# The front of layer 1's attention: waits, loads and order in one engine's list

## What is computed

```python
x = x + _L0_ffn_ref(...)                       # each token: one expert's output, times its weight
y = _L1_cond_ref(x, f, f, w, u, cond)          # sigmoid(x) * (num / den) * (0.8 + 0.2 * tf)
qkv = y @ w_attn + b_attn                      # 16 heads of 32, causal softmax
x = x + (att @ v) @ w_proj + b_proj
```

## Time and profile before

| | us |
|---|---|
| median of 3 runs (2532.3 to 2535.91) | 2533.44 |
| the profiled execution | 2525.72 |
| its span, from first to last instruction | 2524.0 |
| mean granted TensorE clock in it | 0.922 |

### The profile page before, as it was taken

The page is one execution under the profiler, slowest core; times in us unless marked ns, Lnnn a source line. Parts: engine busy times, 40 slices in busy tenths (PEclk is TensorE's granted clock), DMA queues, the critical chain, the costliest instruction groups (busy, mean ns, idle before and its releaser), DMA issues. The chain is left out here.

```text
span 2524.0 us, 43575 instructions
## 1 busy us (share of the span) xinstructions
PE 2093.1 (83%) x14585; PEld 1307.1 (52%) x14585; DVE 1767.6 (70%) x3446; ACT 1355.4 (54%) x3223; POOL 1101.9 (44%) x759
## 2 busy tenths in 40 slices
PE   0678888999999999999995669956789898966999
PEld 0355555565565565566663635533456666643444
DVE  7788877888888878887663449844567767754770
ACT  4566655555555555655553524315476767646442
POOL 5566646555565555554442046633232223210440
PEclk9989988999999999999998579987689899988999
DMA  4233223222122212221122864445333333337110
GB/s 164 80 99 94 80 81 110 76 74 77 60 83 89 70 59 72 78 93 59 56 64 85 334 248 144 144 170 159 102 126 114 102 120 102 118 112 257 34 46 21
DMA packets 112540, 268.53 MB, mean 106 GB/s; under 512 B 10752, under 2 KB 40832, under 8 KB 109824
## 3 DMA queue, kind: packets, MB, share of 16 engines
q1 hardware_dynamic: 93264, 217.50, 25.5%
q10 hardware_dynamic: 16560, 40.64, 4.9%
q0 software_dynamic: 2560, 8.39, 0.9%
HBM read 182.60 MB, written 76.55 MB: 103 GB/s over the span
## 5 line engine op out<-in xcount | busy, mean ns | idle before, releaser
L830 PE MATMUL ps_q<-a_y,a_w 128*128 128x512 f16 x1536 | 356.8, 382 | 0.0
L616 POOL TENSOR_TENSOR a_rb<-a_rb,a_rot 128x512 f32<-128x512 f32 x129 | 187.5, 1454 | 309.0 <-ACT a_rb L729 309.0
L830 PEld LDWEIGHTS ps_q<-a_y,a_w 128*128 128x128 f16 x1536 | 149.8, 102 | 163.8 <-issue 6.1
L620 POOL TENSOR_TENSOR a_qk<-a_ra,a_rb 128x512 f32<-128x512 f32 x129 | 204.6, 1586 | 18.9 <-POOL a_rb L616 0.5
L257 DVE TENSOR_TENSOR_SCAN wkv_bwd<-wk_decay,wkv_tail,wkv_fwd 128x512 f32<-128x512 f32 x114 | 198.5, 1763 | 0.1
L880 PE MATMUL ps_g<-a_o,a_wo 128*128 (+1 forms) x768 | 177.8, 381 | 13.3 <-POOL a_o L607 10.7
L847 PE MATMUL ps_s<-a_qk 128*128 128x512 f32 (+3 forms) x512 | 173.2, 460 | 15.3 <-POOL a_qk L620 15.3
L839 PEld LDWEIGHTS ps_v<-a_w,a_y 128*128 128x128 f16 x3072 | 176.9, 98 | 15.1
L869 PE MATMUL ps_o<-a_tt_,a_v 128*128 128x512 f32 (+3 forms) x512 | 174.6, 488 | 11.1 <-ACT a_tt_ L747 9.5
L839 PE MATMUL ps_v<-a_w,a_y 128*128 128x128 f16 x3072 | 182.0, 219 | 0.0
L968 DVE TENSOR_REDUCE a_nmax<-ps_s 128x1 f32<-128x512 f32 (+3 forms) x256 | 124.7, 487 | 72.1 <-PE ps_s L849 65.4
(11 more groups left out here) (271 smaller groups left out, 4938.6 us busy)
## 6 DMA issues: line engine op xcount, KB each, us to landing
a_w<-wqkv_split SPq DMA_DIRECT2D x48, 768.0 KB, 4.7
scratch_numlog<-wkv_nl ACTq DMA_DIRECT2D x40, 512.0 KB, 2.9
wkv_kt<-in_fT ACTq DMA_DIRECT2D x59, 256.0 KB, 2.7
a_wraw<-in_wqkv SPq DMA_DIRECT2D x18, 768.0 KB, 5.4
wqkv_split<-a_w SPq DMA_DIRECT2D x17, 768.0 KB, 6.8
a_stacks<-qk_parts SPq DMA_DIRECT2D x102, 128.0 KB
gate_up<-in_gate_up SPq DMA_DIRECT2D x8, 1408.0 KB, 14.2
a_nlc<-scratch_numlog SPq DMA_DIRECT2D x18, 512.0 KB, 4.5
```

The costliest lines, as they stand in the source:

```text
L616: pool.tensor_tensor(rb[:, n, :], rb[:, n, :], rot[:, 2 * n + 1, :], ALU.mult).then_inc(s["roped"], 1)
L620: pool.tensor_tensor(qk[:, n, :], ra[:, n, :], rb[:, n, :], ALU.add).then_inc(s["q_sb"], 1)
L830: mm = pe.matmul(psq[n][:], w16[:, i % 2, wp, n, c, :], y16[:, yp, c, :], start=c + m == 0, stop=c == CC - 1 and m == 2)
```

## The change

Four edits, all in `layer1_attn`. The wait for `fixed` and `bq` move from the top of DVE's list to behind the four chunks. `nl0` is loaded in four DMAs, one for each chunk, each with its semaphore, and `xm` is issued behind the first of them. The four first y go to four places (in `ef`), so that `condition` of chunks 1 to 4 no longer waits for `ylo`. In the heads, `weigh` goes ahead of the maxima, and `add_moved` of the tile goes into the next head, behind its maxima.

```diff
+        first_nl = [k.sem(f"a1_first_nl{c}") for c in range(CC)]
...
+        def yf_of(n):
+            return ef[:, 1 - n // 3, n % 3] if isinstance(n, int) and n < CC else yf[:]
...
                 sp.dma_start(x3[:], d["x1"][0].rearrange("c p n -> p c n")).then_inc(s["x1_first"], 16)
-                take_x1(1)
-                sp.dma_start(nl0[:], d["numlog"][2, 0].rearrange("c p m n -> p c m n")).then_inc(s["first_nl"], 16)
+                for c in range(CC):
+                    sp.dma_start(nl0[:, c], d["numlog"][2, 0, c]).then_inc(first_nl[c], 16)
+                    if c == 0:
+                        take_x1(1)
                 sp.dma_start(bqk[:], d["bqkv1"]).then_inc(s["fixed"], 16)
...
-                    pool.tensor_tensor(y[:, 1, c, :], yf[:], y[:, 0, c, :], ALU.subtract).then_inc(s["ylo"], 1)
+                    pool.tensor_tensor(y[:, 1, c, :], yf_of(n), y[:, 0, c, :], ALU.subtract).then_inc(s["ylo"], 1)
...
-                    act.activation(y_of(n)[:, 0, c, :], yf[:], ACT.Copy).then_inc(s["yhi"], 1)
+                    act.activation(y_of(n)[:, 0, c, :], yf_of(n), ACT.Copy).then_inc(s["yhi"], 1)
...
                     if isinstance(n, int) and n < CC:
-                        dve.wait_ge(s["first_nl"], 16)
+                        dve.wait_ge(first_nl[n], 16)
...
                     dve.wait_ge(s["inv"], n + 1)
-                    if not (isinstance(n, int) and n == 0):
+                    if not isinstance(n, int) or n > CC:
                         dve.wait_ge(s["ylo"], n)
-                    conditioned(dve, yf[:], numlog(n)[:, 0, :], wkv_at(b, c), sg[:, side, :]).then_inc(s["yf"], 1)
+                    conditioned(dve, yf_of(n), numlog(n)[:, 0, :], wkv_at(b, c), sg[:, side, :]).then_inc(s["yf"], 1)
...
-                dve.wait_ge(s["fixed"], 48)
-                dve.tensor_scalar(bq[:], bqk[:, 0, :], SCALE, None, ALU.mult).then_inc(s["bq"], 1)
                 weigh(0)
                 for i in range(TT):
                     weigh(i + 1)
...
                     condition(n, n % 2, 0, n)
+                dve.wait_ge(s["fixed"], 48)
+                dve.tensor_scalar(bq[:], bqk[:, 0, :], SCALE, None, ALU.mult).then_inc(s["bq"], 1)
                 take_v(0, 0)
...
+                            if first and h < 2 * TT:
+                                weigh(2 * TT + h)
                             maxima(h + 1, i + 1)
+                            if first and 0 < h <= 2 * TT:
+                                add_moved(2 * TT + h - 1)
...
-                            if first and h < 2 * TT:
-                                weigh(2 * TT + h)
-                                add_moved(2 * TT + h)
```

More of the change, by code:

```diff
@@ L1607, in layer1_attn @@
             "x1_first", "x1_here", "weighted", "moved", "x2", "x2_stored", "wp_raw", "wp64", "wp_hi", "wp_lo",
-            "fixed", "biased", "first_nl", "x_loaded", "sig_step", "sig", "lsum", "inv", "yf", "yhi", "ylo", "y_here",
+            "fixed", "biased", "x_loaded", "sig_step", "sig", "lsum", "inv", "yf", "yhi", "ylo", "y_here",
             "bq", "qproj", "q", "q_hi", "kproj", "k", "k_hi", "qk_low", "parts_out", "stacked", "vproj", "vf", "vhi", "vlo", "scores", "nmax", "expd",
```

## The result

| us | before | after |
|---|---|---|
| median, 4 runs each (2532.3 to 2535.91; 2495.51 to 2509.32) | 2533.38 | 2505.53 |
| the profiled execution | 2525.72 | 2509.32 |
| its span | 2524.0 | 2507.6 |
| mean granted clock | 0.922 | 0.921 |

The ratio is 0.9903 (95% interval 0.9882 to 0.9923, given in brackets from here on): 27.9 us faster by the medians. The two profiled executions differ by 16.4 us only, so the time is followed in them first; what lies between the two numbers comes at the end of the experiments.

The account below looks back on a forecast made before the run. The last stage, from about 1676 us, was taken as the bound: DVE's early waits and PE's waits before moves in the heads. 2525.72 − 8.4 − 0 − 11.2 = 2506.1, plus 7.7 to the median: 2514 us, range 2505 to 2524.

Parts of the forecast that it names:

- The front: Last stage's beginning: weighting starts at 1687.3 in place of 1696.53, so ACT starts the first y 8.4 us earlier.
- `bq` behind the chunks: DVE's wait for the small loads, moved behind the fourth `condition`, near 1710.4: loads landed 14 us before, cost 0.
- Four loads: Division terms in four DMAs: avoids a 0.5 us wait of their first reader, costs nothing; bounds 0 to 3 us lost.
- Four places: Four places for y remove `condition`'s wait for POOL, at most 1.37 us once; taken as 0, bounds 0 to 1.4 gained.
- Head 1's stall: PE's 5.88 us stall ending at 1758.32, covered also by the weight piece and POOL's half: gain 0.
- The other heads: Six other PE waits before moves, 18.1 us at most: gain 11.2 us, middle of 6.4 and 15.9, range 3 to 18.
- Weighting beside POOL's work: Moved weightings in the heads may meet POOL more or less often: 4.1 us later to 2.5 earlier; mean of 795 ns kept.
- Heads gain nothing: Rival: in the heads `values` waits for the addition as long as moves waited for weighting; 2525 us, chance 0.10.
- The clock rises: Rival: PE's clock rises over heads 1 to 8, 10 us more gained; 2504 us, chance 0.06.
- Slower: Rival: waits for the addition keep PE at 1.2 GHz through the eight heads; 2543 us, chance 0.03.
- front fails: Rival: split loads delay gathers or terms by some 8 us at the stage's beginning; 2522 us, chance 0.03.
- The sum: Whole kernel: profiled execution 2525.72 falls to 2506.1; 7.7 us added for the runs' median gives 2514 us.

Follow-up runs that it names:

- the second: The changed kernel run again with nothing edited: median 2504.75 us over 6 runs, ratio 0.9899 against the kernel before.
- the front alone: Changed kernel with weighting and addition back at the end of the head; `bq` late, four loads and four places kept: median 2520.93 us, ratio 0.9958.
- the two profiles above: Two profiles of the changed kernel with the addition at the end of the head: head 3 took 11.21 us at clock 0.54, 9.09 at 0.81.
- the fillers: 24 unread PE multiplications per head in heads 1 to 7, added to the kernel with late `bq`, four loads, four places and old head order: 2524.69 us.
- The two kernels with another place for the addition: Changed kernel with the addition at the end of the head (2500.04 us), or ahead of weighting and maxima in the next head (2497.52 us).

## Why the prediction came out

The forecast was 2514 us, range 2505 to 2524, faster with 0.94. Measured were 2505.5 and 2504.8: faster, by 0.5 us inside the range and by 0.2 outside it. The direction and the mechanisms were right, and two terms were sized too small; that the first median still lies in the range is luck: the range allowed 1 to 2 us for the runs' scatter, and the six runs of the second alone spread over 15.

- **The front, 8.4 us.** ACT came to the first y 9.4 us earlier from the stage's beginning, and the front alone gave 9.4 us by the medians. What failed is "its gathers land at 1692.7: that is what is late next". In this profile the eighth gather had landed when the fifth weighting was ready: of the 6.7 to 7.4 us that a gather takes to land the upper end had been taken, and here the gathers took 6.4 to 6.6. It is a close race all the same: in three of the eight profiles with all of the front's edits the fifth weighting did wait for its gather, 0.3 to 0.4 us (0.40 at 1687.78 in that of the front's edits alone). The first weighting stood at 1687.6, forecast near 1687. At head 0 8.5 us were left of the 9.4, behind transfers that scatter by more.
- **`bq` behind the chunks, 0.** Right: no wait at 1709.50.
- **Four loads, 0.5 us kept and no cost.** The sign was right; one load would have waited 2.3 us and not 0.5, and 0.6 of that reached the fourth chunk's end. The three more issues took 2.12 us of SP and delayed nothing that is seen.
- **Four places, 0, bounds 0 to 1.4.** Right: the wait is 1.4 us, it moves the chunks by 0.6 (without it the fourth `condition` waits 0.57 for ACT and takes 1.23 in place of 0.75), and head 0 shows nothing of it.
- **Head 1's stall, 0.** Right: the stretch that held it, head 2's, took 11.03 us before and after.
- **The other heads, 11.2 us out of 6.4 to 15.9.** Measured 15.1 and 14.2 in the two profiles (and 0.6 in heads 9 to 12), 15.6 by the medians of the heads' edit alone: this is the term that was mis-sized, and most of the miss. The stalls were counted by their own length. Head 3 held a stall of 3.62 us and gave 7.2: behind the stall PE worked on at a low clock (12.34 us busy, then 7.65), and maxima and exponentials waited for its scores. The middle between the two paces left that out, and the clock stood only among the rivals; by the two profiles above it is some 2.1 of head 3's 7.2. Nor was 36.81 the least that four heads can take: heads 1 to 4 took 35.40 with their tiles (heads 5 to 8 38.98), as the pace of heads 9 to 12 held stretches at a low clock itself.
- **Weighting beside POOL's work, mean kept.** 843 ns in place of 795, over seven and eight of them: three are long in both, so no gain and no loss. The contention that the Trainium skill names (GPSIMD Engine Reference, 1. Specifications) is there in single rows, 1.31 us in head 3 before and after. What decides is which of the two instructions starts first, as the last section shows.
- ***Heads gain nothing.*** Its mechanism came true, in part: `values` waits 19.5 us for the addition, nearly as long as the moves had waited, and heads 5 and 6 lose 3.4 us by it. It didn't cost the gain, since in heads 3, 4, 7 and 8, where a wait costs most, 5.1 us of it are left of 13.1. The two kernels with another place for the addition show its price, some 5 us.
- ***The clock rises.*** It rose, to 0.89, and that is part of why the result lies near this rival's 2504. The rule of the Trainium skill (TensorE: Matmul & The Clock Gate, HAM oscillation), that gaps throttle the clock, agrees with the fillers, which raised it from 0.73 to 0.86. The sum of the gaps alone doesn't tell the clock of before from that of after, though: PE waited 24 of 89.5 us at 0.71, and 21.5 of 74.4 at 0.89. And by the fillers the clock was worth about 5 us where the rival took 10, and the fillers' kernel was no faster than the front alone.
- ***Slower*** and ***front fails***: the clock never fell near 0.55 over the eight heads, and the first weighting came before 1690.
- **The sum.** The profile was forecast at 2506.1 and came out at 2509.3: 4.6 us more were gained by head 12 than forecast (24.2 against 19.6), 6.6 were given back behind it, and 1.2 lie ahead of the stage and behind its last head. The 7.7 us added from profile to median were scatter: the profiled execution of before stood below all of its four timed runs, that of after is the slowest of its four, 3.8 above their median.

## What to carry to other kernels

An instruction with a wait at the top of an engine's list costs all that stands behind it, so look what the first wait is for and who needs it first. When an operation is moved ahead of its consumer, follow what its successor then stands behind: here the addition, behind the next weighting, the maxima and a wait for another engine, made `values` late and by it the work of the next head, and gave back some 5 us. Placing it earlier gave the two lowest medians (2497.5 and 2500.0 us), which are not told apart. A stall is priced by the stretch from one mark to the next, clock included, not by its own length; and a sum made on one profile holds that profile's clock too, so compare like stretches at a like clock before explaining a few microseconds.

## What was not expected of the hardware

Two rounds of one loop in one execution took 25.07 us at a granted clock of 1.00 and 27.19 at 0.87, with DVE, ACT and POOL busy for the same time to within 1%. The six runs of one kernel scattered by 15 us, and the longer ones had the lower mean clock (2500.72 and 2500.93 us at 0.927, 2515.87 at 0.923); which of the two makes the other isn't shown.

A weighting beside a POOL instruction is long only where POOL's started first, and then it ends 0.27 to 0.30 us behind that one. This holds for all 43 such rows of the heads in the thirteen profiles: after the change the weighting at 1759.59 took 1.31 us behind a POOL instruction of 1759.28 that ended at 1760.62. The 54 other rows took 0.45 to 0.48 us, also the 24 in which POOL's began during the weighting.

And filling PE's stalls raised its clock from 0.73 to 0.86 over eight heads and shortened them by 5.0 us, yet the whole kernel got no faster by it (2524.7 against 2520.9): in that profile the heads from 12 to 63, which have no fillers, took 385.0 us against 372.4. Why is open.
